# Decoder layer on one core: score maxima in a spare row of the queries, key blocks in halves between silus, a new order on ScalarE

## The reference, cut to what matters

```python
x = x + mamba(layernorm(x), ...)      # conv, silu gate, a scan over 256 steps with 16 states
x = x + xattn(layernorm(x), ctx, ...) # 16 heads of width 8 over 64 context keys, masked softmax
x = x + moe(layernorm(x), ...)        # 8 experts, the best 2 of each token

# xattn
score = einsum('bhqd,bhkd->bhqk', qh, kh) / sqrt(8)
score = where(mask == 0, -1e9, score)
attn = softmax(score)                 # so the maximum of each (query, head) is subtracted
```

## Time and profile before

| | |
|---|---|
| median of 3 runs | 828.12 us (827.78 to 830.49) |
| the profiled execution | 829.39 us, span 827.6 us |
| mean granted TensorE clock | 0.936 |
| busy share of the span | PE 83%, PEld 58%, DVE 83%, ACT 63%, POOL 75% |
| idle time of DVE before its 128 scans and 128 products | 9.0 and 6.0 us |

### The profile page before, as it was taken

One profiled execution on the slowest core, in us unless ns is written; L12 is line 12 of the kernel. 1 busy time (PEld: TensorE's weight loads), 2 busy tenths in 40 slices (PEclk: granted clock), 3 DMA queues, 4 the chain that ended last, 5 costly groups with the idle time before them and its releaser, 6 DMA issues. The chain is left out here.

```text
span 827.6 us, 12373 instructions
## 1 busy us (share of the span) xinstructions
PE 686.6 (83%) x3923; PEld 479.3 (58%) x3923; DVE 684.4 (83%) x1043; ACT 523.0 (63%) x1223; POOL 618.9 (75%) x467
## 2 busy tenths in 40 slices
PE   6578667988898988889888888876679889999993
PEld 3444324556465655546555555554457678899993
DVE  3579999999999999999999999999963564765674
ACT  4677747887976878797687879567133433333345
POOL 1177988977999998999999999999771334675553
PEclk9779878999999999999999999989799999999997
DMA  4534785554648555544753663387254324787765
GB/s 106 205 116 120 211 257 176 164 176 148 190 139 223 167 167 177 181 143 128 224 165 105 193 192 118 114 224 219 69 160 155 126 97 140 249 297 235 228 240 152
DMA packets 80411, 142.70 MB, mean 172 GB/s; under 512 B 10555, under 2 KB 53574, under 8 KB 80346
## 3 DMA queue, kind: packets, MB, share of 16 engines
q1 hardware_dynamic: 75802, 133.38, 52.1%
q0 software_dynamic: 4544, 8.54, 2.9%
HBM read 110.25 MB, written 37.27 MB: 178 GB/s over the span
## 5 line engine op out<-in xcount | busy, mean ns | idle before, releaser
L1526 POOL TENSOR_TENSOR prod<-hst,BC 128x1024 f32<-128x1024 f32 x128 | 301.2, 2361 | 52.9 <-DVE hst L1741 41.8
L1741 DVE TENSOR_TENSOR_SCAN hst<-dA,Rp 128x1024 f32<-128x1024 f32 x128 | 292.3, 2283 | 9.0 <-ACT dA L1222 0.4
L1222 ACT ACTIVATE dA<-dtm,Aneg 128x255 f32<-128x255 f32 x512 | 213.9, 495 | 52.9 <-DVE hst L1741 52.1
L1531 POOL TENSOR_TENSOR prod<-prod 128x512 f32<-128x512 f32 x128 | 161.2, 1270 | 2.4
L1732 DVE TENSOR_TENSOR Rp<-BC,Rp 128x1024 f32<-128x1024 f32 x128 | 156.9, 1226 | 6.0 <-DMA BC<-bcd 0.6
L655 PE MATMUL Y<-prod,ident 128*128 128x256 f32 x512 | 140.5, 407 | 18.1 <-POOL prod L1531 14.6
L1649 POOL DMA_INDIRECT y2d<-prod,back x78 | 77.2, 989 | 97.5 <-DVE prod L2118 80.7
L655 PEld LDWEIGHTS Y<-prod,ident 128*128 128x128 f32 x512 | 101.2, 205 | 55.4 <-POOL prod L1531 20.3
L655 PE MATMUL Mb<-hpad,winT 128*128 128x512 f32 (+1 forms) x176 | 82.2, 615 | 14.7 <-ACT xh L1171 10.4
L1570 POOL DMA_INDIRECT xsd<-x2o,slots x64 | 63.1, 986 | 17.5 <-issue 16.8
L655 PEld LDWEIGHTS Rp<-BC,xh 128*128 128x128 f32 x608 | 73.6, 192 | 3.6 <-issue 1.8
(11 more groups left out here) (289 smaller groups left out, 1134.9 us busy)
## 6 DMA issues: line engine op xcount, KB each, us to landing
BC<-bcd SPq DMA_DIRECT2D x63, 1024.0 KB, 5.6
BC<-recs SPq DMA_DIRECT2D x39, 578.0 KB, 4.0
xsd<-blank SPq DMA_DIRECT2D x17, 1056.0 KB, 11.8
dtm<-xsd SPq DMA_DIRECT2D x39, 132.0 KB, 4.0
recs<-in_L_ffn_W SPq DMA_DIRECT2D x16, 256.0 KB
xin<-in_x SPq DMA_DIRECT2D x8, 256.0 KB, 5.2
x2d<-x2o SPq DMA_DIRECT2D x8, 256.0 KB, 5.6
E<-x2d SPq DMA_DIRECT2D x4, 512.0 KB, 5.4
```

The source lines that it names most:

```text
L1222: m = A(dA[:, k % RING, i, 1:SEQ], dtm[:, r % 2, d, b * SEQ + 1:(b + 1) * SEQ], ACT.Exp, scale=Aneg[:, d, c * NC + i:c * NC + i + 1])
L1526: TT(prod[:, k % RING, :, :], hst[:, k % RING, :, :], BC[:, (k // 2) % BCR, 1, :, :], ALU.mult).then_inc(s_pd, 1)
L1531: TT(prod[:, k % RING, 0:NC // 2, :], prod[:, k % RING, 0:NC // 2, :], prod[:, k % RING, NC // 2:NC, :], ALU.add).then_inc(s_fd, 1)
L1741: v.tensor_tensor_scan(hst[:, k % RING].rearrange("p n s -> p (n s)"), dA[:, k % RING].rearrange("p n s -> p (n s)"), U.rearrange("p n s - ...
```

## The change

1. Maxima. `maxima` writes to columns 64h+32u+j of `mx` (128 wide, zero elsewhere), `split_max` is gone, `turn_max` transposes `mx` in f32, and `copy_max` copies 4 strips of 32 partitions into the rows of `qT` that are zero in version w. `Kbd` gets two versions: version w has -1 in the spare row that holds its head's maximum, so the matmul of keys and queries subtracts it. `scores` uses the other version of both. The mask is transposed once in round 0 (`turn_mask`, `copy_mask`); `scores_t` then has four matmuls with the keys and four for the mask.
2. Keys. Eight scaled and shifted copies in place of four, in halves: one ahead of each gate silu (`key_half`).
3. ACT's order: `twice_contexts` from step 5 to 3, `att_out` and `mixer_out` from 5 to 4, `spreads` and `att_square` to 5, `att_inverse_root`, `decays(r, 10)` and `expert_exps` ahead of the silus at 6, the decays of steps 7 to 12 one step earlier, `inverse_roots_x` and `copy_xh(r+1, 0)` to step 14 around `copy_max`, both `exps` to 15.
4. PE: `att_variance` between `conv(r+1, 1)` and `gate_in`. `turn_max` waits for the last maximum.
5. DVE: `logits` from the middle of step 6 to the middle of step 5. `inputs` of step 14 no longer waits for `split_max`.

```diff
             def turn_max(r):
-                pe.wait_ge(Tv.sem, Tv.at("me", r))
+                pe.wait_ge(Tv.sem, Tv.at("mx3b", r))
                 for i in range(NB * QT):
-                    m = pe.transpose(Tb[0:96, i * P:(i + 1) * P], nm[:, i, :, :], identb[:, :])
+                    m = pe.transpose(T[0][:, i * P:(i + 1) * P], mx[:, i, :], ident[:, :])
...
                 for i in range(2):
                     for h in range(2):
-                        o, hp = T[h][:, i * SEQ:(i + 1) * SEQ], TRIO[g][h][i]
-                        mm(o, selmax[:, hp, :], nmT[:, b * SEQ:(b + 1) * SEQ], start=False, stop=False, skip_group_check=True)
-                        for t in range(QT):
-                            m = mm(o[:, t * P:(t + 1) * P], mbias2[:, t, :, :], identb[:, :], start=False, stop=True,
-                                   skip_group_check=True)
+                        rows = slice(64 * h, 64 * h + 64)
+                        m = mm(T[h][:, i * SEQ:(i + 1) * SEQ], twice[rows, :, :], mbiasT[rows, :], start=False, stop=True,
+                               skip_group_check=True)
...
                     if k == (5 if r else 6):
                         conv(r + 1, 1)
+                        if prev:
+                            att_variance(r - 1)
                         gate_in(r + 1)
...
                 for d in range(DT):
+                    if between:
+                        key_half(r - 2, d)
                     act.wait_ge(Ap.sem, Ap.at(f"rs{d}", r))
                     A(sres[:, r % 2, d, :], M[d], ACT.Silu).then_inc(Aa.sem, 1)
...
+            def key_half(r, w):
+
+                if w == 0:
+                    act.wait_ge(Ta.sem, Ta.at("KT", r))
...
+                for j in range(HP // 2):
+                    m = A(Kbd[:, w, :, j, :], KT[:, :, :], ACT.Identity, bias=kshift[:, w, j:j + 1], scale=kscale[:, w, j:j + 1])
+                if w == 1:
+                    m.then_inc(s_kb, 1)
...
             def copy_max(r):
                 act.wait_ge(Tp.sem, Tp.at("m", r))
-                A(nmT[:, :], Tb[0:96, 0:NB * SEQ], ACT.Copy).then_inc(Ta.sem, 1)
+                for w in range(2):
+                    for h in range(2):
+                        rows = slice(64 * h + 32 * (1 - w), 64 * h + 32 * (2 - w))
+                        m = A(qT[rows, w, :, :].rearrange("p b s -> p (b s)"), T[0][rows, :], ACT.Copy)
+                m.then_inc(Ta.sem, 1)
...
-                if k == 6 and r < ROUNDS:
+                if k == 6:
                     copy_xh(r, 1)
                 if prev and k == 6:
-                    key_blocks(r - 1)
-                    att_square(r - 1)
+                    if not nxt:
+                        key_blocks(r - 1)
+                    att_inverse_root(r - 1)
+                if k == 6:
+                    decays(r, 10)
+                if tail and k == 6:
+                    expert_exps(r - 2)
                 if nxt and k == (6 if r else 7):
-                    silus(r + 1)
+                    silus(r + 1, bool(r))
...
+                g = r * STEPS + k + (4 if 7 <= k < 13 else 3)
+                if k != 13 and g < ROUNDS * STEPS:
                     decays(*divmod(g, STEPS))
...
...
...
                 if tail:
+                    if k == 5:
                         logits(r - 2)
```

More of the change, by code:

```diff
@@ L328, in decoder @@
         Ta = Marks(sem("Ta"), "KT V sq ln rs q m e00 e01 e10 e11 ld rd x2")
-        Tv = Marks(sem("Tv"), "xq " + " ".join(f"mx{i}a mx{i}b" for i in range(NB * QT)) + " ma mb mc md me n")
+        Tv = Marks(sem("Tv"), "xq " + " ".join(f"mx{i}a mx{i}b" for i in range(NB * QT)) + " n")
         s_kb = sem("s_kb")
+        s_mk = sem("s_mk")
         s_cT = sem("s_cT")
@@ L913, in slot @@
                         steps_in(r + 1)
-                if prev and k == 5:
+                if prev and not nxt and k == 5:
                     att_variance(r - 1)
@@ L1000, in _, with turn_mask @@
             mm(T[0][:, SEQ:SEQ + 1], attT[:, 3, :], bv[:, :]).then_inc(s_tr, 1)
+            def turn_mask():
+                pe.wait_ge(s_k, 3)
+                pe.wait_ge(s_cT, 2)
+                for t in range(QT):
+                    m = pe.transpose(Tb[:, t * P:(t + 1) * P], mbias2[:, t, :, :], identb[:, :])
+                m.then_inc(s_mk, 1)
             def first_round(k):
@@ L1165, in scan_input, with silus @@
                 A(hpad[:, :, TAPS - 1:], xn2[:, :].rearrange("p (b s) -> p b s", b=NB), ACT.Identity, bias=lnb[:, 0:1]).then_inc(Aa.sem, 1)
-            def silus(r):
+            def silus(r, between=False):
                 for d in range(DT):
@@ L1260, in copy_kv @@
                 m.then_inc(Ta.sem, 1)
-            def key_blocks(r):
[L1264 to L1270, removed]
-                m.then_inc(s_kb, 1)
+            def key_half(r, w):
+                if w == 0:
+                    act.wait_ge(Ta.sem, Ta.at("KT", r))
+                    if r:
+                        act.wait_ge(Tp.sem, Tp.at("st11", r - 1))
+                    else:
+                        act.wait_ge(s_pre, NPRE + 12)
+                for j in range(HP // 2):
+                    m = A(Kbd[:, w, :, j, :], KT[:, :, :], ACT.Identity, bias=kshift[:, w, j:j + 1], scale=kscale[:, w, j:j + 1])
+                if w == 1:
+                    m.then_inc(s_kb, 1)
+            def key_blocks(r):
+                key_half(r, 0)
+                key_half(r, 1)
             def copy_max(r):
                 act.wait_ge(Tp.sem, Tp.at("m", r))
-                A(nmT[:, :], Tb[0:96, 0:NB * SEQ], ACT.Copy).then_inc(Ta.sem, 1)
+                for w in range(2):
[3 more added lines that the diff above has]
+                m.then_inc(Ta.sem, 1)
             def exps(r, b, g):
@@ L1373, in slot @@
                     square_x(r + 2)
+                if ln and k == 14:
+                    inverse_roots_x(r + 2)
                 if prev and k == 14:
                     copy_max(r - 1)
-                if ln and k == 14:
-                    inverse_roots_x(r + 2)
-                if prev and k >= 14:
-                    exps(r - 1, 0, k - 14)
+                if nxt and k == 14:
+                    copy_xh(r + 1, 0)
+                if prev and k == 15:
+                    exps(r - 1, 0, 0)
+                    exps(r - 1, 0, 1)
             def drain(r, k):
@@ L1944, in _ @@
             nxt_(v.tensor_copy(identb[:, :], ident[:, :]))
-            nxt_(v.tensor_copy(selmax[:, :, :].rearrange("p g (h k) -> p (g h) k", h=2), pickmax[:, :].unsqueeze(2).to_broadcast([96, HEADS, KEYS])))
+            for h in range(2):
+                half = slice(64 * h, 64 * h + 64)
+                nxt_(v.tensor_copy(twice[half, :, :], ident[half, half].unsqueeze(1).to_broadcast([64, 2, KEYS])))
             v.wait_ge(s_prea, 1)
```

85 lines of the change are left out of this document (35 added, 50 removed).

## The result

| | before | after |
|---|---|---|
| median | 828.88 us (827.78 to 830.49, 4 runs) | 847.87 us (847.09 to 848.99, 4 runs) |
| profiled execution, span | 829.39, 827.6 us | 848.64, 846.5 us |
| last scan starts at | 602.0 us | 620.9 us |
| mean granted clock | 0.936 | 0.916 |

The ratio is 1.0243, with a 95% interval of 1.0218 to 1.0267. The kernel became 19 us slower. The forecast was 11 us slower and the range ended at 847: the direction was right, the size wrong. The profiled executions differ by 18.9 us, and all of it is there by the last scan. The stretch behind it has the same length in both, 225.6 us.

The account below looks back on a forecast made before the run. DVE bounds the rounds (68.7 of 71 us busy), PE what follows. 829.39 - 9.1 + 19.1 + 3.9 - 1.0 - 1.2 = 841.1 us, as median 839.5; own range 834 to 845 (0.64), 8 in 10 from 830 to 847.

Parts of the forecast that it names:

- The split is gone, 9.1 us less.: DVE after the last maximum: without five instructions the next product starts at once, 1.3 us in each of rounds 1 to 7.
- The logits, 19.1 us more.: DVE in step 5 waits for PE's router matmuls: 3.6 us in four rounds, 2.2 in round 5, 2.5 in round 6.
- rival (3): PE's chain starts late ahead of `normalise`, up to 2 us in six rounds: 852 us in the median; chance 0.13.
- one of the prediction's own signs of being wrong: The prediction called itself wrong if, among other signs, `oT` comes before PE has done its conv.
- ACT's new order, 3.9 us more.: Root, decays and key copies delay ACT's queries, so DVE waits at the maxima: 3.9 us, from 0 to 8.
- Had the logits not moved, undoing one loss alone gains little.: Without the early logits, ACT's chain to the queries would become the wait instead, 3 us a round.
- What ACT has more elsewhere is beside idle time.: Three more copies of the maxima cost nothing in the rounds, as ACT waited 52.1 us for DVE's scans.
- PE's cheaper scores and the copies, 2.2 us less behind the last scan.: Cheaper `scores_t` calls against dearer transposes and copies: -1.0 us after the rounds, -1.2 us in the drain.
- The drain's share, 1.2 us: In the drain, the split's wait of 0.7 and four cheaper calls saved, against transposes and copies: -1.2 us.
- (1): PE at full clock in every round, so each loses 2.2 us like round 5: 830 us in the median; chance 0.11.
- (2): No wait for the logits at step 5, only the removed work counts: 817 us in the median; chance 0.07.
- (4): POOL is the bound, so only 2.2 us after the rounds are gained: 826 us in the median; chance 0.05.

Follow-up runs that it names:

- the last kernel: Kernel before with only the new maxima, key blocks' second half behind step 10's decays, first half in quarters among the silus: 820.55 us, ratio 0.9914.
- The kernel with only the maxima: Kernel before with only the new maxima (no split, spare rows, four copies, eight key blocks), logits and engine orders as before: 856.0 us, ratio 1.0338.
- the mask experiment: The one with only the new maxima, with the mask matmuls of each transposed-score call issued twice: 856.16 us against 856.0.
- decays and exponentials put back: Changed kernel with step 10's decays and the experts' exponentials back behind the silus, the root staying ahead: 845.06 us, ratio 1.0189.
- silus first: Changed kernel with ScalarE's silus ahead of the inverse root, step 10's decays and experts' exponentials in rounds 1 to 6: 841.36 us, ratio 1.0141.

## Why the prediction was wrong

- *The split is gone, 9.1 us less.* Right as work, and the last kernel has it as a gain (9.5 us by the last scan). But it is one only where ScalarE has room for what replaces it.
- *The logits, 19.1 us more.* Right in mechanism, releaser and place. VectorE waited 2.50, 2.49, 3.10, 2.99, 2.99 and 4.15 us in rounds 2 to 7. The idle time grew by 16.2. Rounds 2 to 4 lost less than the 3.6 counted each: PE had its full clock there (granted 1.00 from `oT` to the mark, and 7.0 to 7.2 us for that stretch, where the kernel before had 0.81 and 9.0 in round 2). Round 5 lost more than 2.2 (it waited 2.99), as PE reached `att_out` late: the first matmul of `att_out` came at 417.72 without a wait, after conv, though `oT` was done at 417.07. That is rival (3) in small, 0.65 us, and one of the prediction's own signs of being wrong. The same is seen in rounds 4 and 6 (0.8 and 0.65 us).
- *ACT's new order, 3.9 us more.* **This is the step that failed.** The sum followed ScalarE to the queries and asked only when the scores would be there. The 3.9 us that it put at the maxima were 1.3 (0.22 in round 5 for 0.8). It left out that PE stands in `gate_in` in the meantime, with `sum_states` of the next steps behind it: the first silu's delay goes by PE, POOL's ring and Y to the gate. The prediction put nothing there, and the runs showed 13.5 us. I had named what is queued behind VectorE's new wait, and not what is queued behind PE's old one, which grew from 2.24 to 6.17 us (10.4 to 38.0 in all). PE's slower matmuls behind that stall, 1.80 us a round, were not in the sum either. Of the key copies in this term the size was right: a second pointer column cost 96 ns a copy (483 - 387), more than the 78 read from the earlier trace rows.
- *Had the logits not moved, undoing one loss alone gains little.* Right in size (2.7 us by the medians), wrong in place: the gate and not the queries took most of it over.
- *What ACT has more elsewhere is beside idle time.* The outcome held in the changed kernel (VectorE does not wait for the scan's input there), the reason did not. In round 5 before, ScalarE waited for no scan from `copy_max` to the scan's input, so the 52.1 us of the earlier trace rows were in other steps. The kernel with only the maxima shows what that means: 16.8 us of new waits at the scan's input, and 14.5 at the root for the key blocks. ScalarE's new order is what hides them.
- *PE's cheaper scores and the copies, 2.2 us less behind the last scan.* Measured 0: 225.6 us in both. Four copies took 2.39 us (forecast 2.05) and the four transposes 0.66 (0.60). Against the forecast of one call at the lower clock, three ran slow, behind a longer idle time of PE (2.48 us, and 1.18 between the first calls). A call's masks at the higher clock took 0.38 us, in the forecast's 0.23 to 0.46. The drain's share, 1.2 us, was not measured by itself.
- *Rivals.* The condition of (1) did occur in five of six rounds: PE at full clock from `oT` to the logits' mark in rounds 2 to 6, at 0.81 only in round 7. It is the main reason why the logits' term came out at 16.2 for 19.1. Its 830 did not come, as the loss at the gate stood beside it. (2) and (4) didn't occur. The sum by waits: -9.1 + 16.2 + 13.5 + 1.3 (maxima) - 4.2 (root of attention 0.8, root of x 2.8, scan's input 0.6 less) = 17.7 us of the 18.9. Against the forecast's 841.1 for the profiled execution, 13.5 us at the gate were left out and 2.2 behind the last scan were not gained; 2.9 at the logits, 2.6 at the maxima and 4.2 at other waits were too much. That makes 6.0 of the 7.5 us. The forecast came as near as it did because these errors partly cancel, which is luck.

Open: why the kernel before with early logits takes 856 to 862 us in three executions and 846 in one. The granted clock differs between them (0.937 and 0.913 to 0.917), and the mask experiment does not decide whether that is cause or effect. Open too is how much of the gate's wait is due to PE's stall and how much to the slower matmuls behind it. The latter alone don't bring it (with the decays and exponentials put back, the four matmuls took 3.78 us in round 5 and the gate did not wait), but no run has the long stall without them.

## What to carry to other kernels

An instruction that is made late holds its waiter's whole queue: list for each engine what stands behind every wait that grows, old ones too. Work taken from the busiest engine is a gain only where the engine that receives it has room at that step; look at its timeline around the steps that others wait for, not at its share. If a change comes out slower, fit its useful part by itself: here it was worth 7 us in the median when its extra work stood in the receiver's own waits. Do not expect a removed wait to come back as time in full: here 13.5 us of waiting gave 7 us in one kernel and about 3 in another, as later waits grew.

## What the hardware showed beside it

- A copy by ScalarE from PSUM on 32 partitions took as long as one on 96 or 128: 588 ns for 32x512, 593 for 96x512, 580 for 128x512 (`x2o<-T`). Cut into four strips, the maxima's copy took 2.39 us.
- The same four matmuls of 512 columns took 1.98 us after 2.24 us of waiting and 3.78 after 6.17 (0.50 us and 0.95 each). In the window of the latter the granted clock was 0.50, the lower level, 1.2 GHz, and it was 1.00 in the former. The other rounds bear this out: 1.98 or 1.99 us behind each wait of up to 2.24 us (the kernel before and "silus first"), from 1.98 to 3.78 behind one of 3.44 (decays and exponentials put back), and 3.78 behind each of 6.17. So the long stall was paid for twice, in waiting and in slower matmuls.
- 128 more mask matmuls, 6.7 us of PE's busy time, went with a mean granted clock of 0.926 for 0.917 and no change in time. More than half of the rise was behind the scans, where it went from 0.95 to 0.97.
